# A four-layer graph network: wide comparisons and additions moved behind the logits in the first edge pass

## The reference

```python
# layer 0: attention with one logit per edge
h_trans = x @ W_att.T + b ; logits = leaky(h_trans[src] @ a_src + h_trans[dst] @ a_dst)
h_neigh = segment_sum(softmax_by_dst(logits) * (x @ W1.T + b1)[src], dst)
# layer 1: four-head attention: Q[dst]·K[src] + edge bias, softmax by dst, sum of V[src]
# layer 2: edge MLP: e = silu(silu([h[row], h[col]] @ We1) @ We2); agg = segment_sum(e, row)
# layer 3: two graph convolutions: out = segment_sum(h[row] * norm, col)
x = layernorm(x + layer(x))        # after each
```

## Time and profile before

| | |
|---|---|
| runs, us | 6945.59, 6977.82, 6950.0 (median 6950.0) |
| profiled execution, span | 5685.5 us, 82572 instructions |
| profiled execution, its own time | not recorded; the median run is 1264.5 us above the span |
| busy shares of the span | POOL 70%, DVE 57%, PE 55%, PE weight load 48%, ACT 26% |
| granted TensorE clock, first pass | 0.51 of full speed |

### The profile page before, as it was taken

How to read it: one execution, slowest core, us unless ns; L and a number is a source line. 1 busy time by engine, 2 the same in 40 slices (tenths; PEclk the granted TensorE clock), 3 DMA queues, 4 the chain that set the end, 5 groups by cost and what they waited for, 6 DMA issues and landing times. The chain is left out here.

```text
span 5685.5 us, 82572 instructions
## 1 busy us (share of the span) xinstructions
PE 3113.8 (55%) x17051; PEld 2734.5 (48%) x17052; DVE 3263.6 (57%) x12090; ACT 1491.5 (26%) x5626; POOL 3958.0 (70%) x4054
## 2 busy tenths in 40 slices
PE   4444444356666666778898988433333443333333
PEld 3333333345555555657777776333333343333332
DVE  6888887676787787744444444433444443344445
ACT  2333333345555555532222223100000000000001
POOL 3777777736777777367777772677777757777774
PEclk7555555568888777865555556666666666666666
DMA  5111112214444444222121110111111121111112
GB/s 123 52 52 52 52 52 56 49 52 131 132 132 131 130 131 131 70 54 56 52 56 51 53 52 21 56 52 51 51 51 51 51 61 52 51 51 51 51 51 57
DMA packets 222234, 385.68 MB, mean 68 GB/s; under 512 B 85452, under 2 KB 121882, under 8 KB 221998
## 3 DMA queue, kind: packets, MB, share of 16 engines
q0 software_dynamic: 142944, 296.35, 19.0%
q1 hardware_dynamic: 79054, 86.72, 5.0%
HBM read 356.23 MB, written 26.56 MB: 67 GB/s over the span
## 5 line engine op out<-in xcount | busy, mean ns | idle before, releaser
L2246 POOL DMA_INDIRECT arena<-table_gcn,idx_now x1568 | 1532.2, 977 | 642.9 <-issue 422.1
L2296 PE MATMUL pair<-arena,hotf 128*128 x3328 | 726.6, 408 | 1224.7 <-POOLq L1819 1199.3
L2296 PEld LDWEIGHTS pair<-arena,hotf 128*128 128x128 f32 x3328 | 691.2, 317 | 1256.1 <-issue 1255.8
L664 POOL DMA_INDIRECT arena<-table_attention,idx_now x832 | 825.7, 992 | 272.7 <-issue 197.2
L664 POOL DMA_INDIRECT arena<-table_key_value,idx_now x832 | 789.2, 949 | 275.9 <-issue 221.1
L1852 POOL DMA_INDIRECT arena<-table_edge_mlp,idx_now x784 | 768.1, 980 | 261.2 <-issue 212.4
L2323 DVE TENSOR_TENSOR acc<-acc,pair 128x1024 f32 x208 | 253.9, 1221 | 1133.9 <-PE pair L2299 1133.9
L1069 PE MATMUL pair<-wide,hotf 128*128 128x130 f32 x1664 | 431.0, 439 | 653.3 <-ACT wide L1033 653.3
L1069 PEld LDWEIGHTS pair<-wide,hotf 128*128 128x128 f32 x1664 | 369.0, 326 | 718.5 <-ACT wide L1033 718.5
L2256 ACT COPY idx_now<-src_t 128x8 int32 (+1 forms) x204 | 39.3, 197 | 1815.2 <-PE pair L2299 1803.2
L1406 PE MATMUL pair<-wide,hotf 128*128 128x132 f32 x1664 | 314.1, 347 | 232.9 <-DVE acc L1436 232.8
(11 more groups left out here) (371 smaller groups left out, 5709.7 us busy)
## 6 DMA issues: line engine op xcount, KB each, us to landing
key<-rel_dram SPq DMA_DIRECT2D x104, 256.0 KB, 3.4
arena<-rel_dram SPq DMA_DIRECT2D x52, 512.0 KB, 3.7
arena<-table_gcn,idx_now POOLq DMA_INDIRECT x1568, 2.5
arena<-table_attention,idx_now POOLq DMA_INDIRECT x832
arena<-table_key_value,idx_now POOLq DMA_INDIRECT x832
arena<-table_edge_mlp,idx_now POOLq DMA_INDIRECT x784, 2.4
table_attention<-arena SPq DMA_DIRECT2D x13, 512.0 KB, 3.0
table_gcn<-acc SPq DMA_DIRECT2D x26, 256.0 KB, 2.3
```

The lines of the kernel that those rows point to most:

```text
L664: q_.indirect_dma_start(ring[:, slot, 0:width], None, table, bass.IndirectOffsetOnAxis(ap=idx_now[:, slot:slot + 1].bitcast(U32), axis=0)) ...
L2246: q_.indirect_dma_start(conv_ring[:, slot * D:(slot + 1) * D], None, table, bass.IndirectOffsetOnAxis(ap=idx_now[:, slot:slot + 1].bitcast ...
L2296: t_.matmul(window[:, bass.ds(offset * D, D)], hot8[:, g % 2, u, :], conv_ring[:, bass.ds(slot * D, D)], start=False, stop=False)
```

## The change

Five edits:

1. First pass: the four comparisons of a group become one `tensor_tensor` of 128x512 elements, with the row 0..127 and the node numbers both broadcast from SBUF (`hots(g)`, the helper that the second pass uses).
2. First pass: all four additions stand behind the logits of the group, one behind the other, and belong to group k-3 instead of k-2; after the last group three groups are left over instead of two.
3. First pass: a third pair of PSUM banks takes part (`l0_bank`: pairs 0, 1 and 3 in turn), and PE waits for one group of additions less. The sort's one late matmul moves from pair 3 to pair 2.
4. Third pass: the eight comparisons of a group become one `tensor_tensor` of 128x1024 elements.
5. `rows_of` puts the loaded number through one more register operation (maximum with 0), on DVE in the third pass and on PE in the convolutions.

```diff
+        def l0_bank(k, u):
+            return pair[(0, 1, 3)[k % 3]][:, u // 2 * 512 + u % 2 * AW:u // 2 * 512 + u % 2 * AW + D + 2]
...
-                                              in1=pair[3][:, :].rearrange("q (b p) -> q b p", **by_block), op0=ALU.mult, op1=ALU.add))
+                                              in1=pair[2][:, :].rearrange("q (b p) -> q b p", **by_block), op0=ALU.mult, op1=ALU.add))
...
-                    add = back(*later(i, g, -2)) if past >= 2 else lambda u: None
+                    add = back(*later(i, g, -3)) if past >= 3 else lambda u: None
                     nodes = nodes_of(dve, regs, g)
                     dve.wait_ge(l0_placed, k + 1)
-                    for u in range(G):
-                        v.tensor_scalar(out=hotf[:, g, u, :], in0=iota[:, :], scalar1=rel_now[:, g * G + u:g * G + u + 1], scalar2=None,
-                                        op0=ALU.is_equal)
-                    add(0)
+                    v.tensor_tensor(out=hotf[:, g, :, :], **hots(g))
                     for u in range(G):
                         last = v.scalar_tensor_tensor(out=junk[:, 0, u * P:(u + 1) * P], in0=iota[:, :],
...
-                        if u == 1:
-                            add(1)
                     ch(last)
-                    add(2)
                     arrived(dve, i, g)
                     ch.wait()
                     ch(v.tensor_add(lg[:, g, 0, 0:G], ring[:, g * G:(g + 1) * G, D + 1], small[:, g, G:2 * G]))
-                    add(3)
                     ch.wait()
                     v.scalar_tensor_tensor(out=lg[:, g, 1, 0:G], in0=lg[:, g, 0, 0:G], scalar=0.01, in1=lg[:, g, 0, 0:G],
                                            op0=ALU.mult, op1=ALU.max).then_inc(l0_logit, 1)
+                    for u in range(G):
+                        add(u)
...
-                for g in range(RING - 2, RING):
+                for g in range(RING - 3, RING):
...
-                        last = t_.matmul(bank[6 + h], pick_last[:, :], last_tile[:, h * 512:(h + 1) * 512], start=True, stop=True)
+                        last = t_.matmul(bank[4 + h], pick_last[:, :], last_tile[:, h * 512:(h + 1) * 512], start=True, stop=True)
...
-                    pe.wait_ge(l0_acc[G - 1], k + 1)
+                    pe.wait_ge(l0_acc[G - 1], k)
...
-            eng.reg_load([need], table[0:1, bass.ds(k, 1)])
-            return eng.snap(need, min_val=0, max_val=CTILE_GROUPS - 1) + 1
+            loaded, bounded = need
+            eng.reg_load([loaded], table[0:1, bass.ds(k, 1)])
+            eng.reg_alu(bounded, loaded, 0, ALU.max)
+            return eng.snap(bounded, min_val=0, max_val=CTILE_GROUPS - 1) + 1
...
-                    for u in range(CG):
-                        last = v.tensor_scalar(out=hot8[:, g % 2, u, :], in0=iota[:, :], scalar1=rel_now[:, g * CG + u:g * CG + u + 1], scalar2=None,
-                                               op0=ALU.is_equal)
-                    last.then_inc(l2_same, 1)
+                    v.tensor_tensor(out=hot8[:, g % 2, :, :], in0=iota[:, :].unsqueeze(1).to_broadcast([P, CG, P]),
+                                    in1=rel_now[:, g * CG:(g + 1) * CG].unsqueeze(2).to_broadcast([P, CG, P]), op=ALU.is_equal).then_inc(l2_same, 1)
```

More of the change, by code:

```diff
@@ L964, in add @@
                             dve.wait_ge(l0_acc[G - 1], k + 2)
-                        v.tensor_add(here, here, bank[2 * (g % 2) + u // 2][:, (u % 2) * AW:(u % 2) * AW + D + 2]).then_inc(l0_acc[u], 1)
+                        v.tensor_add(here, here, l0_bank(k, u)).then_inc(l0_acc[u], 1)
                     return add
@@ L1066, in step @@
                     pe.wait_ge(l0_wide, k + 1)
-                    pe.wait_ge(l0_acc[G - 1], k + 1)
+                    pe.wait_ge(l0_acc[G - 1], k)
                     for u in range(G):
-                        last = t_.matmul(bank[2 * (g % 2) + u // 2][:, (u % 2) * AW:(u % 2) * AW + D + 2],
-                                         hotf[:, g, u, :], wide[:, g, u, 0:D + 2], start=True, stop=True)
+                        last = t_.matmul(l0_bank(k, u), hotf[:, g, u, :], wide[:, g, u, 0:D + 2], start=True, stop=True)
                     last.then_inc(l0_sum, 1)
@@ L1975, in _ @@
                 slots = [dve.alloc_register(f"l2_slot{u}") for u in range(CG)]
-                need = dve.alloc_register("l2_need")
+                need = [dve.alloc_register(f"l2_need{n}") for n in range(2)]
                 def hot_look(i, g, k):
@@ L2281, in _ @@
                     offsets = [pe.alloc_register(f"{name}_offset{u}") for u in range(CG)]
-                    need = pe.alloc_register(f"{name}_need")
+                    need = [pe.alloc_register(f"{name}_need{n}") for n in range(2)]
                     def step(i, g, k):
```

## The result

The changed kernel takes **6922.7 us** (median of 7 runs, 6901.9 to 6926.1); the kernel before takes 6958.7 in the 7 runs beside it. Ratio 0.9944, 95% interval 0.9927 to 0.9961: faster by 36 us, or 0.56%. The forecast was 6966.

A forecast was written before the change was run, and what follows sets the result against it. The prediction took POOL's issuing of gathers to bound the first pass and the two behind it. Its terms, 12 + 0 + 0 + 1 + 3 + 0 = +16 us on 6950, gave 6966 us, range 6925 to 7025.

The forecast's parts named there:

- an instruction less on DVE is worth nothing by itself: All passes: DVE's work counts only if it exceeds POOL's pace or lengthens POOL's instructions; saved DVE work priced at 0.
- the 40 us of edit 1: First pass: DVE saves 208 x 0.2 = 40 us, worth 0 beside POOL; port price 12, ends 0 and 20.
- the 0.44 us a group of edit 4: Third pass: one wide comparison saves DVE 0.44 us a group, worth 0 beside a 5 us wait.
- POOL waiting over 60 us for ACT's indices: Sign named as showing the forecast wrong, in favour of rival 3.
- rival 3: First pass: DVE becomes the bound, 5.3 us a group against POOL's 5.0 plus stalls; up to 7000 us; no separate chance.
- The 1264.5 us: Whole run: time taken as outside the profiled span of 5685.5 us, left unchanged and added to reach 6950 us.
- The 1.59 us: First pass: four additions in a row behind the logits cost DVE 1.59 us, each waiting for the one before.
- the 5.3 us of DVE's cycle: First pass, sorting groups: DVE's cycle grows from 4.45 to 5.3 us, against POOL's 5.0 to 5.2; priced at 0.
- The sort pairs' share: First pass: sort pairs move 0.9 us later; their share of 36 us gather surplus taken as unchanged, range -25 to +30.
- The terms for the port: Third pass: wide comparison stalls gathers, +19 us; `hot_look` moves earlier and stalls fewer, -16; sum +3.
- Rival 1: Third pass: wide comparisons start ahead of gathers and hold the port, +107 us, about 7065; chance 0.22 for over +35.
- Rival 2: First and third pass: the port comes free, gather surplus of 24 + 36 us goes, 6890 us; chance 0.10 for over -35.

The follow-up runs named there:

- e8: Kernel before plus the register operation and one unread 128x512 comparison a group in 192 first-pass groups; ratio 0.9992, on the 5668 us chip.
- e2: Kernel before plus the register operation and the first pass's wide comparison; ratio 0.9945 against the kernel before at 6956 us.
- e11: Kernel before plus the register operation and the wide comparisons of first and third pass; 6862 us, ratio 0.9876 against the kernel before at 6950 us.
- e18: The kernel of e11 run again: register operation and both wide comparisons on the kernel before; 6875 us, ratio 0.9889.
- e5: The kernel of e11 (register operation and both wide comparisons on the kernel before) on the 5668 us chip; ratio 1.0048.
- e7: Kernel before plus register operation, first pass's wide comparison and one unread 128x128 comparison a group in 192 groups; ratio 1.0028, on the 5668 us chip.
- e17: Kernel before plus register operation, first pass's wide comparison, additions behind the logits and third bank pair; ratio 0.9995 against the kernel before at 6950 us.
- e6: The kernel of e17 (the whole change without the third pass's wide comparison) on the 5668 us chip; ratio 1.0047 against the kernel before.
- e1: Kernel before plus the register operation alone; ratio 0.9998 against the kernel before at 6956 us.

## Why the prediction was wrong

- **What bounds the kernel.** The step that failed is "an instruction less on DVE is worth nothing by itself". It was right for the profile I had, and e8 shows it (some 110 us added, nothing lost). With it every term of saved work was put at 0, the 40 us of edit 1 and the 0.44 us a group of edit 4. It is wrong on the chips that timed the change: VectorE pauses there, POOL's lead of four groups is used up every 25 to 30 us, and POOL waits in the first pass 235 us for ACT's indices (33 in the earlier trace rows). There saved work was worth up to its own length: 38 us for edit 1 alone, which makes VectorE 43 us less busy (e2), 86 and 77 for edits 1 and 4 (e11 and e18; 43 and 36 us less busy in the two passes of e11). The prediction had named "POOL waiting over 60 us for ACT's indices" as a sign against it, as rival 3's; but what it was a sign of is the pauses, which no rival had.
- **The 1264.5 us.** I put them before and behind the traced instructions without any row for it. Every term that was priced at 0 because it is hidden beside POOL rests on a profiled execution 18% shorter than the timed ones, and it was one that had run in another manner. I should have given such a case a chance of its own.
- **Edit 1** (forecast +12): -38 us (e2). The gathers grew by 29 us, but the wide comparison lengthened only some 8 us of them (7 in the whole change); the rest is the shifted sort pairs. All of it was outweighed by fewer waits. On the 5668 chip the first pass moved by -10 (e5) to +9 (e7), so the ends 0 and +20 were a little high there.
- **Edit 2** (forecast 0, ends -25 and +36): alone nothing that can be told, but with edit 1 it takes back what edit 1 gives (e17), and costs 22 us on the 5668 chip (e6 against e5). The 1.59 us were right, and the 5.3 us of DVE's cycle as well: the undisturbed step from logits to logits is 5.2 in the changed kernel. That a longer cycle could count was in rival 3. The sort pairs' share, taken as unchanged, is 22 us in the whole change and 25 in the profile of before.
- **Edit 3** (forecast +1): never run apart from edit 2; its share stays open.
- **Edit 4** (forecast +3, ends -22 and +107): some -22 us in the third pass on the 6950 chips; on the other +31 against e8, +14 against the profile of before, whose third pass took 1006. The terms for the port can be told apart in the whole change: 59 gathers behind the wide comparison make 42 us (forecast 19), and `hot_look` fell from 23 to 8 us (forecast -16, right). On the slow chips this lies beside POOL's waits and cost nothing. Rival 1 had the mechanism (starts ahead of POOL's) and the 5668 chip paid nearly a third of its 107 us.
- **Edit 5** (0): right, 0.9998. It wasn't run alone on the 5668 chip. There the third pass took 989 to 991 us in the three kernels that change nothing else in it (e6 to e8) and 1006 in the profile of before; `hot_look` lengthens fewer gathers in them.
- **Rival 2** had the right sign for a wrong reason, so its 0.10 was no foresight: no port came free, as the gathers of the first and third pass are longer than e1's (986 and 1008 ns against 975 and 964). And by the prediction's own reading of the port, the wide comparison with its two SBUF inputs takes it too.
- **The signs.** Of those named as right, the row of additions at 1.59 us came in, and long gathers that end some 0.8 us behind a wide comparison. The others did not: the first pass's gathers had a mean of 986 ns (995 to 1010 was named), the third's 1008 (975 to 990), the second's 976 where 949 was to stay, and of VectorE's 195 us before the logits only 10 are put down to rows (60 to 110 was named).
- **The sum** +16 with 0.10 for faster: on the 5668 chip the parts add up to more than it (e5's 27 and the 22 of the additions, about 50 us). Whether the whole change is slower there was not run and is open. That 6922.7 lies only 2 us below the forecast's range says nothing for the terms: the sum had the wrong sign.

**Open:** what the pauses are. Shown is that they come with the chip (or its condition) and not with the change, that VectorE and in the convolutions PE have them, that POOL's gathers go on through VectorE's (520.97 to 525.96 in e1), and that gathers, clock and the instruction packets seen don't account for them. Other ways in which an instruction could come late are not ruled out. Not settled is why instructions taken away pay more than instructions added cost, nor what edits 2 and 3 do to the gain of edit 1. POOL's counts of waits stand on one profile of each run.

## What to carry to other kernels

Compare the span of a profile with the timed runs before anything else; where they differ by hundreds of us, as here, what it shows as hidden may not be hidden in the runs that count. Merging short instructions of the engine that drains a ring can pay even when that engine is idle a third of the time, if the ring's lead is being used up by something else. Test the parts of a change apart: here edits 2 and 3 took back over half of what the others gave. And where two engines share a port, look also at which of the unchanged instructions the edit moves onto the start of a gather (here the sort pairs). On a chip where POOL's issue is the bound, check the same merge for starts just ahead of a gather.

## What the runs showed of the hardware that I had not expected

- The same kernel takes 5668 us on one chip and 6950 to 6968 on three others, with the same instructions and the same granted clock in the first pass (0.51 and 0.52). What the traces show beside that are the pauses.
- In a pause VectorE takes an instruction about every 1.4 us, even one without any wait (620.59, 621.99, 623.39 of the changed kernel), and the longest one shown here lasts 9 us (519.85 to 528.65 in e1).
- A bf16 128x1024 `tensor_scalar` holds up a gather that began up to 0.25 us before it (45 in the profile of before), a 128x512 fp32 `tensor_tensor` does not, even when it begins 0.01 us behind.
- One more 128x512 comparison in 192 groups, some 110 us of busy time, costs nothing on either kind of chip (0.9992 and 0.9983), although taking 43 us away gives 38 on one of them.
